# Masks of other lanes kept in DRAM between attention layers instead of made on VectorE in each

## What is computed

```python
def _gat_layer(x, src, dst, ea, W, We, a_src, a_dst, a_edge, b, n):
    h = x @ W
    e = ea @ We
    s = (h @ a_src)[src] + (h @ a_dst)[dst] + e @ a_edge
    s = jax.nn.leaky_relu(s, NEG_SLOPE_ATT)
    smax = jax.ops.segment_max(s, dst, num_segments=n)
    ex = jnp.exp(s - smax[dst])
    denom = jax.ops.segment_sum(ex, dst, num_segments=n)
    out = jax.ops.segment_sum(h[src] * (ex / denom[dst])[:, None], dst, num_segments=n)
    return out + b
```

## Time and profile before

| | us |
|---|---|
| median of three runs | 13679.91 |
| the profiled execution | 13686.51 |
| its span | 13684.8 |
| first attention layer, with what stands ahead of it | 0 to 2153 |
| attention layers 1 to 3, each with the gap behind it | about 2050 |
| last attention layer with its gap | 2112 |
| EdgeConv | 10509 to the end |

### The profile page before, as it was taken

How to read it: one execution, slowest core, us unless ns; L and a number is a source line. 1 busy time by engine, 2 the same in 40 slices (tenths; PEclk the granted TensorE clock), 3 DMA queues, 4 the chain that set the end, 5 groups by cost and what they waited for, 6 DMA issues and landing times. The chain is left out here.

```text
span 13684.8 us, 304796 instructions
## 1 busy us (share of the span) xinstructions
PE 9345.4 (68%) x64194; PEld 8215.7 (60%) x64195; DVE 8876.7 (65%) x23089; ACT 6472.5 (47%) x12901; POOL 9449.1 (69%) x10337
## 2 busy tenths in 40 slices
PE   6888886666666666666666666666665555657999
PEld 6888885555555555555555555555554555554699
DVE  4667776666776666776666776666775444446787
ACT  5555664444444444444444444444444222225887
POOL 3777776777775777775777775777774777773266
PEclk7878887888888888888888888888887778788999
DMA  4222222222222222222222222222222444446754
GB/s 101 54 54 54 54 54 49 54 54 54 54 56 49 54 54 54 54 56 48 54 54 54 54 56 57 54 54 54 54 53 52 108 110 112 115 117 201 220 147 136
DMA packets 905699, 1019.87 MB, mean 75 GB/s; under 512 B 535592, under 2 KB 589063, under 8 KB 905482
## 3 DMA queue, kind: packets, MB, share of 16 engines
q0 software_dynamic: 300288, 630.00, 21.3%
q1 hardware_dynamic: 517362, 256.23, 7.7%
q10 hardware_dynamic: 87848, 131.57, 2.8%
HBM read 875.68 MB, written 142.21 MB: 74 GB/s over the span
## 5 line engine op out<-in xcount | busy, mean ns | idle before, releaser
L969 POOL DMA_INDIRECT rows<-node_table,idx x9384 | 8883.7, 947 | 3363.9 <-issue 2924.7
L1200 PE MATMUL bank<-ident,u_edge 128*128 128x128 f32 x8800 | 2145.1, 323 | 3182.8 <-DVE u_edge L1061 3177.4
L1200 PEld LDWEIGHTS bank<-ident,u_edge 128*128 128x128 f32 x8800 | 1380.3, 157 | 3768.3 <-DVE u_edge L1061 2735.9
L1234 PE MATMUL bank<-rows,work 128*128 x17600 | 3011.9, 326 | 33.1 <-ACT work L1319 19.1
L1234 PEld LDWEIGHTS bank<-rows,work 128*128 128x128 f32 x17600 | 2765.9, 239 | 104.1 <-issue 100.3
L1300 ACT ACTIVATE work<-bank,v_low 128x512 f32<-128x512 f32 x2200 | 1511.8, 687 | 2542.6 <-PE bank L1202 1940.3
L1074 DVE SCALAR_TENSOR_TENSOR work<-bank,acc,work 128x512 f32<-128x512 f32 x1760 | 1321.1, 751 | 1601.1 <-issue 1593.3
L1202 PE MATMUL bank<-mask_ident,other_lane 128*128 128x128 bf16 x8800 | 1898.1, 244 | 0.0
L1081 DVE TENSOR_REDUCE group_top<-work 128x1 f32<-128x512 f32 x2200 | 1508.4, 686 | 271.4
L1213 PE MATMUL bank<-ident,work 128*128 128x128 f32 x8800 | 1654.3, 321 | 0.0
L1056 DVE SCALAR_TENSOR_TENSOR other_lane<-bank,group_base,dst_of 128x512 bf16<-128x512 f32 x2200 | 1632.0, 742 | 9.9 <-issue 5.5
(11 more groups left out here) (283 smaller groups left out, 11846.1 us busy)
## 6 DMA issues: line engine op xcount, KB each, us to landing
rows<-edge_features SPq DMA_DIRECT2D x831, 256.0 KB, 2.8
rows<-node_table,idx POOLq DMA_INDIRECT x9384
edge_features<-work ACTq DMA_DIRECT2D x440, 256.0 KB
work<-in_edge_attr SPq DMA_DIRECT2D x48, 256.0 KB, 3.3
node_table<-acc ACTq DMA_DIRECT2D x147, 65.0 KB
idx<-sources_by_quad SPq DMA_DIRECT2D x150, 32.0 KB
node_table<-hx SPq DMA_DIRECT2D x7, 458.5 KB, 4.4
node_table<-hx SPq DMA_DIRECT2D x1, 3209.5 KB, 22.2
```

The costliest lines, as they stand in the source:

```text
L969: nc.gpsimd.indirect_dma_start(rows[:, s, q * TW:(q + 1) * TW], None, tables[layer % 2], bass.IndirectOffsetOnAxis(ap=idx[:, half, s, q:q ...
L1200: nc.tensor.matmul(bank[r][:, q * P:(q + 1) * P], u_edge[:, r, q:q + 1].broadcast_to([P, P]), ident[:, :], start=True, stop=False, is_tran ...
L1234: ins = nc.tensor.matmul(bank[4 + r][:, 0:P + 1], att[:, r, q * P:(q + 1) * P], rows[:, at(slot), q * TW:q * TW + P + 1].rearrange("p a w ...
```

## The change

In the first layer the mask is still made on DVE, and ACT stores each one to a new tensor in DRAM (`store_mask`, 128 KB each). In the four later layers DVE no longer makes it: ACT issues a load of the mask of group i + 8 into the turn that group i has just left (`load_mask`, after `logits_made` of group i); the last 8 steps of layers 1 to 3 load the first eight masks of the next layer (`load_next_mask`), and the first eight of layer 1 are loaded behind the steps of layer 0. PE waits for the landing in `logits`. The semaphores `feat_landed` are shared with EdgeConv, where the counts waited for grow by what the masks add.

```diff
@@ DRAM tensors
+    masks_dram = nc.dram_tensor("other_lanes_by_group", [NG, P, GE], BF16, kind="Internal").ap()
@@ helpers
+        MASKS = 2 * NG
+        def mask_of(i):
+            return masks_dram[at(i), :, :].rearrange("a p e -> p (a e)")
@@ attend, DVE
                 def edge_side(i, k):
                     quad, slot = now["quad"], now["slot"]
-                    if first and past(i, UN):
-                        dve.wait_ge(lanes_hot, i - (UN - 1))
-                    nc.vector.scalar_tensor_tensor(out=other_lane[:, k, :].rearrange("p (q c) -> p q c", c=P),
-                                                   in0=lanes_by_tile, scalar=base_of(i), in1=quad_dst(quad),
-                                                   op0=ALU.add, op1=ALU.not_equal)
+                    if first:
+                        if past(i, UN):
+                            dve.wait_ge(lanes_hot, i - (UN - 1))
+                            dve.wait_ge(feat_landed[k], i * 2 - k * 2)
+                        nc.vector.scalar_tensor_tensor(out=other_lane[:, k, :].rearrange("p (q c) -> p q c", c=P),
+                                                       in0=lanes_by_tile, scalar=base_of(i), in1=quad_dst(quad),
+                                                       op0=ALU.add, op1=ALU.not_equal)
@@ attend, PE, logits
                     pe.wait_ge(u_made, g0 + i + 1)
+                    if not first:
+                        pe.wait_ge(feat_landed[k], i * 2 + (layer * MASKS + 16 - k * 2))
@@ attend, ACT
+                def store_mask(i, k):
+                    act.wait_ge(u_made, g0 + i + 1)
+                    stand_alone(act, "act")
+                    act.dma_start(mask_of(i), other_lane[:, k, :]).then_inc(feat_landed[k], 16)
+                def load_mask(i, k):
+                    act.wait_ge(logits_made, g0 + i + 1)
+                    stand_alone(act, "act")
+                    act.dma_start(other_lane[:, k, :], mask_of(i + UN)).then_inc(feat_landed[k], 16)
+                def load_next_mask(i, k):
+                    act.wait_ge(logits_made, g0 + i + 1)
+                    stand_alone(act, "act")
+                    act.dma_start(other_lane[:, k, :], mask_of(i + UN - NG)).then_inc(feat_landed[k], 16)
...
                 if first:
-                    stages = groups((1, low), (0, exps), (-2, copy_att), (-2, hot_lanes))
+                    stages = groups((1, low), (0, exps), (-2, copy_att), (-2, hot_lanes), (-2, store_mask))
                 elif last:
-                    stages = blocks((-ACT_LAG, copy_rows), (-5, relu_rows)) + groups((1, low), (0, exps)) \
+                    stages = blocks((-ACT_LAG, copy_rows), (-5, relu_rows)) + groups((1, low)) \
+                        + [(1, load_mask, 0, NG - UN)] + groups((0, exps)) \
                         + blocks((-5, copy_turned)) + groups((-2, copy_att))
                 else:
-                    stages = blocks((-ACT_LAG, copy_rows)) + groups((1, low)) + blocks((-6, copy_mixed)) \
+                    stages = blocks((-ACT_LAG, copy_rows)) + groups((1, low)) \
+                        + [(1, load_mask, 0, NG - UN), (1, load_next_mask, NG - UN, NG)] + blocks((-6, copy_mixed)) \
                         + groups((0, exps)) + blocks((-5, copy_turned)) + groups((-2, copy_att)) \
                         + blocks((-ACT_LAG, store_rows))
                 staged_pipeline(act, UN, stages, fetch)
+                if first:
+                    act.wait_ge(logits_made, NG)
+                    act.wait_ge(lanes_hot, NG)
+                    for k in range(UN):
+                        act.wait_ge(feat_landed[k], MASKS)
+                        act.dma_start(other_lane[:, k, :], mask_of(k)).then_inc(feat_landed[k], 16)
@@ EdgeConv, ACT, two places
-                    act.wait_ge(feat_landed[k], 16 * (turn + 1))
+                    act.wait_ge(feat_landed[k], L * MASKS + 16 * (turn + 1))
```

More of the change, by code:

```diff
@@ L2040, in relu @@
                 def relu(i, k, turn):
-                    act.wait_ge(feat_landed[k], 16 * (len(range(k, NQ, 8)) + turn + 1))
+                    act.wait_ge(feat_landed[k], L * MASKS + 16 * (len(range(k, NQ, 8)) + turn + 1))
                     if past(i, 2):
```

## The result

The changed kernel takes 13649.26 us (median of 19 runs, 13637.42 to 13659.66), the kernel before on the same chip 13683.41 (19 runs, 13676.59 to 13687.69): 34 us less, a ratio of 0.9976 with a 95% interval of 0.9969 to 0.9982. The forecast was 13639 with a range of 13595 to 13674. The time is inside it and counts as faster by the prediction's bound of 0.2%, but two steps of the working were off: the first layer costs 19 us more than was said, and 8.4 us of gain came that the sum did not count.

The account below looks back on a forecast made before the run. POOL's gathers were taken to bound the layers, DVE's sequencer the steps at their ends. Gains of 27, 10 and 6 us less 2.5 made 40.5 off the median 13679.9: 13639 us, range 13595 to 13674.

Parts of the forecast that it names:

- What bounds the kernel: Inside a layer POOL's gathers bound, 1.25 us each; only the last 40 or so steps of layers 1 to 4 can gain.
- The step at a layer's end: Ends of layers 1 to 4: DVE's sequencer sets the step; 0.17 us saved in each of 158 steps, 27 us.
- The wait before L1114: At a layer's end, DVE's "issue" idle time there grows by about 0.5 us, to 0.8 and 1.5.
- Waits for the others: Ends of layers 1 to 3: DVE's waits for PE and ACT shrink, 3.3 us per layer, 10 us gained.
- Rival 2: At layer ends the PE and ACT chain takes back DVE's gain; only 10 us gained, 13670 us; chance 0.22.
- Start of the backlog: Just ahead of the blocks in later layers, DVE falls behind later: 1.5 us per layer, 6 us gained.
- ACT's load and the landing: Later layers: ACT's about 0.6 us per step is covered, and masks asked for 8 groups ahead land in time; no cost.
- The first layer: Layer 0: gathers bound it too, stores are issued under L1327, eight end loads follow; 2.5 us lost.
- Rival 4: Loop code: last layer's DVE stall ends, 8.4 us gained, chance 0.15; or ACT's loops stall, some 28 us lost, chance 0.05.
- Rival 3: Mask loads beside the gathers lengthen them; 0.04 us per load makes 70 us, 13709 us; chance 0.07.
- The sum: Whole kernel: 27 + 10 + 6 - 2.5 = 40.5 us gained.

Follow-up runs that it names:

- loads_alone: Changed kernel storing only the first layer's last eight masks, without DVE's wait for their landing; all loads read those eight: 13623.85 against 13672.6 us for the kernel before.
- four_both: Changed kernel with stores and loads four masks per DMA: 17307.18 against 17343.06 us on a 17.3 ms chip, 13614.73 against 13677.5 us on one like the first.
- four_stores: Changed kernel with the first layer's masks stored four per DMA and DVE waiting in two of eight steps: 17301.1 against 17343.06 us, ratio 0.9976.

## Why the prediction was right, and where not

**What bounds the kernel: right.** The inner layers kept their length but for the gathers' pace, and the gain of the later layers lies in their gaps.

**The step at a layer's end: right.** 0.17 us per step was said. Undisturbed steps went from 4.62 and 5.22 us to 4.44 and 5.04, 0.18 less, in layer 4 from 5.44 and 6.04 to 5.26 and 5.86. Two experiments show the cause: 0.40 us less datapath alone brings 3.0 us over all four gaps, and slots alone bring the old steps back. The wait before L1114 was to grow by about 0.5 us, here L1122 (8160 to 8330):

```profile
L1139 DVE SCALAR_TENSOR_TENSOR hot<-hx 128x128 f32<-128x128 f32 x34 | 10.0, 294 | 7.9 <-ACT hx L1376 7.9
...
L1122 DVE RECIPROCAL share<-acc 128x1 f32 x34 | 5.6, 164 | 34.6 <-issue 34.6
```

It grew from 0.74 (28.0 us in 38) to 1.02 us only. In this layer L1139 (the old L1131) also waits 0.23 us for ACT in place of 0.07, but that is not the reason: in layer 2, where L1139 doesn't wait, L1122 has 1.02 too, and an undisturbed pair of 0.69 and 1.29 where 0.8 and 1.5 were said.

**Waits for the others: the size came out by luck.** 10 us were said to come from waits that end. 43 steps at the ends of layers 1 to 4 became 7.1, 14.6, 5.7 and 16.3 us shorter, 43.7 in all. Less 28 for 158 steps of 0.18 and 8.4 for the loop, 7 are left. They are a balance: layer 2, which had the slow beat before (rows above, 3.8 us of waiting), lost it and gained 14.6, and layer 3 kept it and gained 5.7. So a wait ended in one layer and one was gained in another. Layer 1 had the fast beat before and after, and its gap fell by 9.1 us. The gap of layer 3 is 90 and not 80 us because L1139 waits there. Layer 2 (6090 to 6294) and layer 3 (8121 to 8334) of the changed kernel:

```profile
L1139 DVE SCALAR_TENSOR_TENSOR hot<-hx 128x128 f32<-128x128 f32 x39 | 11.4, 293 | 0.2
...
L1139 DVE SCALAR_TENSOR_TENSOR hot<-hx 128x128 f32<-128x128 f32 x40 | 11.8, 294 | 9.0 <-ACT hx L1376 8.8
```

Two beats are possible, with and without that wait, and the kernels that make masks have both as well. `loads_alone` has the slow one in layer 2 (88.1 us) and not in layer 3, the kernels with four masks per DMA have it nowhere. Rival 2's chain exists, then, and costs about 10 us where it catches. What decides it was not found.

**Start of the backlog: right.** 6 us were said. DVE's `u_edge` waits for landings up to the blocks again (8060 to 8120, in place of none in rows 6), and 44 groups before the end it came 1.65 to 2.1 us behind SyncE's signal before and 0.3 after, 6.6 us over the four layers:

```profile
L1069 DVE TENSOR_TENSOR u_edge<-rows,late 128x4 f32 x15 | 2.5, 167 | 1.4 <-SPq L935 1.3
```

**ACT's load and the landing cost nothing: right** within 1 to 4 us per layer's end, by the run without loads and by the one with a quarter of their instructions.

**The first layer: the step that failed.** "It is bound by its gathers too" was inferred from the other layers, with no row of layer 0 behind it. For its stream it is right (2022.4 us before, 2019.7 after, the difference being the gathers' pace), but not for its end, where DVE runs behind. The row says 0.17 us of reserve per step. ACT's half of the edit was costed at nothing under its L1327, and DVE's wait got no price but "looks 8 groups back", which is right for what it waits for and leaves out the instruction itself. DVE's sequencer sets the step there as at the other ends, and the prediction had priced such an instruction at 0.094 us, on the side of the gain only. It cost 21.7 us in place of 2.5, of which 2.1 are the eight loads that the 2.5 stood for (with the last eight stores).

**Rival 4, first half, came true:** 8.4 us from the stall (three steps of 8.9, 8.8 and 8.6 us became 5.8 each, less the 0.5 that they gained as steps), given a chance of 0.15. Its second half (ACT's loops begin to stall) did not: ACT's loops of 230 and 240 records turn in 0.20 to 0.22 us.

**Rival 3 did not come:** the gathers have 944 ns with loads, with stores, with both and with neither (947 in the kernel before as profiled; more on that below).

**The sum.** Said: 43 in the later layers less 2.5. Measured in the profile pair: 48.8 less 21.7, 27.1 us from the gaps. The sum of 40.5 is 13.4 too high by the gaps, 19.2 for the first layer less 8.4 for the loop, and 2.6 for the rest. The time lies only 10 us above the forecast, and that is in part luck. The 8.4 of the loop came unforecast. And 7 us between these 27 and the medians' 34 stay open; the gathers' pace, below, is the one thing seen that could give them. Against them stand 3.5 us by which the kernel before is slower here than in the three runs that the forecast starts from.

## What to carry to other kernels

A cost that is "hidden" is hidden by a reserve, and the reserve has a row: sum the waits of the engine for the resource that bounds the stretch, divide by its steps, and compare with every instruction that the change adds to that step, in each stage by itself. Price an instruction on an engine whose sequencer sets the step the same way whether it is taken out or put in; work in 4 steps' batches where it can be batched, since here two stores and two waits per eight steps in place of eight of each were worth 17.5 us at the first layer's end with the same bytes. Before two gaps are compared, see whether the same wait stands in both: here one that is on in one layer and off in another was worth up to 10 us. And when a loop has some 270 records or more, look at its turns after any edit, also of code that comes before it.

## What the runs showed of the hardware

- One more wait in each step of layer 0 went with a stall of a DVE loop of 271 records in layer 2: about 4.5 us more idle time at each of three turns, 13 to 16 us in all, nearly half of what the change gained.
- The same text can have two paces of its gathers. `four_both` and `four_both_2` are one kernel; their gather rows on two chips are these:

```profile
L970 POOL DMA_INDIRECT rows<-node_table,idx x9384 | 8882.6, 947 | 6858.7 <-SPq L941 3600.3
```

```profile
L970 POOL DMA_INDIRECT rows<-node_table,idx x9384 | 8862.3, 944 | 3308.4 <-issue 2922.9
```

  3 ns make some 21 us of a kernel. The 21.6 us of the profile pair need therefore be no effect of the change.
- On the 17.3 ms chips the gathers are as quick, yet POOL waits for free slots. POOL between 6500 and 7500, `four_stores` and then the changed kernel:

```profile
L970 POOL DMA_INDIRECT rows<-node_table,idx x617 | 582.1, 943 | 419.1 <-SPq L941 255.0 <-issue 164.1
```

```profile
L970 POOL DMA_INDIRECT rows<-node_table,idx x802 | 756.8, 944 | 244.4 <-issue 244.4
```

  TensorE's granted clock has a mean of 0.75 in place of 0.82 there, and POOL stands still for 2.85 us at 6406.6, for one. The cause is open. The change, with its stores in fours, is worth 0.2% there.
- DVE's loads of registers from SBUF took longer near one of ACT's DMA issues (1.16 against 0.97 us, 0.41 against 0.34). Overlap with a load of ACT's alone did not lengthen them (0.97 and 0.34 in the kernel before).
